# A four-layer graph network on one core: the row gathers unrolled on GpSimd, with a deeper ring in two layers

## The chip, the cores and the metric

The kernel runs on 1 core of one Trainium2 chip. The metric is device time in microseconds (us), from the runtime, for one execution. The engines have the names of the profile: PE (TensorE), DVE (VectorE), ACT (ScalarE), POOL (GpSimd) and SP (SyncE, which here only issues DMAs).

## The reference, cut to what matters

The graph has 6250 nodes of 128 float32 features and 106250 edges, sorted by destination. Four layers run one after the other, each on `h = relu(layernorm(x))`, and each adds its result to `x`:

```python
# layer 0: attention          per edge: k[src], v[src] (two rows of 128), q[dst]
a = einsum('eho,eho->eh', kw[src], q[dst]) * pri;  attn = softmax of a over the edges of a dst
h_agg = segment_sum(m * attn, dst)
# layer 1: degree-normalised  per edge: xs[src] (one row of 128)
h = segment_sum(xs[src], dst) * norm_out
# layer 2: gated              per edge: x[src] @ W_src and x[src] @ W_msg (two rows), edge_attr
gates = sigmoid(x_row @ W_src + x_col @ W_dst + edge_attr @ W_edge)
out = segment_sum(x_row @ W_msg * gates, dst) / segment_sum(gates, dst)
# layer 3: mean (SAGE)        per edge: x[src] (one row of 128)
summed = segment_sum(x[src], dst)
```

## The kernel before, in words

The edges lie in `T` = 896 tiles of 128 edges; every tile holds edges of one block of 128 destination nodes. Four tiles are a group (`QUAD`), so there are `NQ` = 224 groups. The node tables that are read per edge lie in device memory: `tab2` with rows of 1024 bytes (layers 0 and 2, the stages `scores` and `gated` in the code) and `tab1` with rows of 512 bytes (layers 1 and 3, the stages `degree` and `mean`).

In every layer POOL fetches the source rows: one indirect DMA for each tile (L500, 4 for a group, 896 for a layer, 3584 in all) takes 128 row numbers from a column of SBUF and brings 128 rows into the buffer `G`. `G` is a ring of `RING` = 4 groups. The row numbers of all tiles lie in `SRC`, one column for each tile; SP copies the four columns of a group by a small DMA into `ISLOT`, which has the same ring of 4 (L576, in layer 0 L596), and POOL names the columns of `ISLOT`. So before the gathers of group q POOL waits for the copy (`idx_filled`, L494), for the reader of the slot to be done with group q-4 (`rows_read`, L495), and in layer 0 for the store of the slot's second half (`mv_stored`, L497).

The loops of a layer's groups are made by `steps`: the first 8 groups and the last 8 are written out, those between run in a loop (`Fori`) whose body is 8 groups. Layer 0 has its own `layer0_steps`, which lets the messages of a group follow its scores 40 groups later, and has 7 hooks, one after every 32 groups, in which DVE works out the running maxima (`maxima`).

What reads the gathered rows: in `scores` DVE multiplies the first half of the rows with the spread q (L1257), and SP stores the second half (v) to `mvd` in device memory (L593) and loads it back into `MV` when the messages are due (L604; DVE weighs it, L1264). In `degree` and `mean` PE reads the rows directly: DVE makes a one-hot matrix for each tile (L971), PE multiplies it with the rows (L688, `pe_agg`), and DVE adds the four results to the accumulator of the block (L988). In `gated` DVE adds the first half (L1339) and multiplies the second half with the gate (L1331), then PE and DVE aggregate as before. The order in every engine's queue is written by hand, and all waits are semaphores. In `degree` DVE also makes two bf16 one-hots (L947, L951) for a histogram that PE sums (L702).

SP's queue, in order: in layer 0 for each step first the wait for the gathers of group q-4, their store to `mvd` and the index copy of group q, then the load of `MV`; in `degree` and `mean` only index copies, behind the loads of the next layer's weights (L645 to L648, L656 to L660); in `gated` the index copy and four loads of edge attributes (L580) for each group.

Of the kernel before, what the change touches and what calls it, by code (L numbers as in the profile page):

```python
# [7 lines left out]
I32 = mybir.dt.int32  # L8
# [13 lines left out]
RING = 4  # L22
UNROLL = 8
# [38 lines left out]
def build(nc, sz, a):  # L62
# [3 lines left out]
    with ctx:  # L66
        def sb(name, shape, dt=F32):
            return ctx.enter_context(nc.sbuf_tensor(name, shape, dt))

        def sem(name):  # L70
            return ctx.enter_context(nc.semaphore(name))
# [26 lines left out]
        ISLOT = sb("ISLOT", [P, RING, QUAD], I32)  # L98
# [27 lines left out]
        G1 = G[:, 0:RING * QUAD * D].rearrange("p (r j d) -> p r j d", r=RING, j=QUAD)  # L126
# [12 lines left out]
        def edge_sems(n):  # L139

            s = {"onehot_ready": sem(f"onehot_ready_{n}")}
            if n != "scores":
                s |= {k: sem(f"{k}_{n}") for k in ("agg_done", "rows_added")}
            if n != "messages":
                s |= {k: [sem(f"{k}{r}_{n}") for r in range(RING)] for k in ("idx_filled", "gathered")}
            return s
# [4 lines left out]
        def at(i, u, d):  # L151

            v = u + d
            i = i + v // UNROLL if v // UNROLL else i
            v %= UNROLL
            return i * UNROLL + v, v % RING, i * (UNROLL // RING) + v // RING, v

# [331 lines left out]
        def pool_gathers(pool, n, rows, table):  # L489
            s = ps[n]  # L490

            def step(i, u):
                q, slot, turn, _ = at(i, u, 0)
                pool.wait_ge(s["idx_filled"][slot], (turn + 1) * 16)  # L494
                wait(pool, rows_read[n], q - RING + 1)  # L495
                if n == 0:
                    wait(pool, mv_stored[slot], turn * 16)  # L497
                pool.sem_inc(may_gather, 1)
                for j in range(QUAD):
                    nc.gpsimd.indirect_dma_start(  # L500
                        out=rows[:, slot, j, :], out_offset=None, in_=table,
                        in_offset=bass.IndirectOffsetOnAxis(ap=ISLOT[:, slot, j:j + 1], axis=0),
                    ).then_inc(s["gathered"][slot], 16)
            steps(pool, step, 0)
# [64 lines left out]
        def sp_edges(sp, n):  # L569

            s = ps[n]

            def step(i, u):
                q, slot, turn, _ = at(i, u, 0)
                wait(sp, s["gathered"][slot], turn * 64)
                sp.dma_start(ISLOT[:, slot, :], SRC[:, bass.ds(q * QUAD, QUAD)]).then_inc(s["idx_filled"][slot], 16)  # L576
                if n == 3:
                    wait(sp, gated["pre_done"], q - RING + 1)
                    for j, first in enumerate(registers(sp, SROW, q, sz.edge_end)):
                        sp.dma_start(EA[:, slot, j, :], a["ea_t"][:, bass.ds(first, P)]).then_inc(ea_loaded[slot], 16)  # L580
            steps(sp, step, 0)

        def sp_layer0(sp):

            s = ps[0]

            def step(i, u, scores, messages):
                q, slot, turn, _ = at(i, u, 0)
                if scores:
                    wait(sp, s["gathered"][slot], turn * 64)  # L590
                    if not isinstance(q, int) or RING <= q < NQ + RING:
                        sp.sem_inc(may_move, 1)
                        sp.dma_start(mvd[bass.ds(q - RING, 1), :, :].rearrange("o p (j d) -> (o p) j d", j=QUAD),  # L593
                                     G2[:, slot, :, D:2 * D]).then_inc(mv_stored[slot], 16)
                    if valid(q):
                        sp.dma_start(ISLOT[:, slot, :], SRC[:, bass.ds(q * QUAD, QUAD)]).then_inc(s["idx_filled"][slot], 16)  # L596
                if messages:
                    q, slot, turn, _ = at(i - LAG, u, 0)
                    if valid(q):
                        sp.wait_ge(mv_stored[slot], (turn + 1) * 16)  # L600
                        sp.sem_inc(may_move, 1)
                        wait(sp, weighted["weighted"], q - RING + 1)
                        sp.sem_inc(may_move, 1)
                        sp.dma_start(MV[:, slot, :, :].rearrange("p j d -> p (j d)"),  # L604
                                     mvd[bass.ds(q, 1), :, :].rearrange("o p f -> (o p) f")).then_inc(mv_loaded[slot], 16)

            def guarded(i, u, scores, messages):
                step(i, u, scores and not (isinstance(i, int) and i == sz.iters and u >= RING), messages)
            layer0_steps(sp, guarded)
# [5 lines left out]
        def _(sp):  # L615
# [33 lines left out]
            sp_edges(sp, 2)  # L649
# [4 lines left out]
            sp_edges(sp, 3)  # L654
# [6 lines left out]
            sp_edges(sp, 4)  # L661
# [29 lines left out]
        def pe_plain(pe, n):  # L691
# [3 lines left out]
            def step(i, u):  # L695
# [8 lines left out]
                pe.wait_ge(s["gathered"][slot], (turn + 1) * 64)  # L704
                pe_agg(pe, n, q, slot, v % 2, lambda j: G1[:, slot, j, :], D)
# [721 lines left out]
```

## Time and profile before

| | us |
|---|---|
| median of 3 runs | 5664.36 |
| lowest and highest | 5662.23, 5675.72 |
| span of the profiled execution | 6742.5 |
| busy in it: POOL, DVE, PE, ACT | 3636.2, 3229.3, 3183.9, 663.9 |

The profiled execution is one execution under the hardware profiler; of its own time the page gives the span alone, from the first to the last instruction. It is 1078 us longer than the median of the runs without it. Each digit below is the busy share of 1/40 of the span in tenths; `PEclk` is TensorE's granted clock in tenths of full speed. The four stages with gathers are where POOL's digits are high.

```profile
PE   4534445444453333333426777677775133333333
DVE  6345665666785434343455444444446422322225
POOL 3465555555601666666653555555553366666661
PEclk9767676766766555555558888888887555555556
DMA  2345445555521111111223444444443111111131
```

### The profile page before, as it was taken

How to read it: one execution, taken by the hardware profiler on the slowest of the kernel's cores; microseconds unless marked ns; L12 is line 12 of the kernel's file. 1: busy time of each engine (PE TensorE's matmuls, PEld its weight loads, DVE VectorE, ACT ScalarE, POOL GpSimd, SP SyncE). 2: the span in 40 equal slices, each digit the busy share in tenths (PEclk: the TensorE clock that was granted, in tenths of full speed). 3: DMA queues.
4: the chain of work that ended last, by engine and by line, in shares of the span. 5: the costliest groups of instructions: out<-in, count | busy, mean ns of one | idle time of the engine just before them, and what ended most of it. 6: DMA issues, size and time to landing. Idle time of an engine off the chain costs nothing. (4 is left out here: it accounts for less than half of the span.)

```text
span 6742.5 us, 78555 instructions
## 1 busy us (share of the span) xinstructions
PE 3183.9 (47%) x16832; PEld 2674.3 (40%) x16833; DVE 3229.3 (48%) x7806; ACT 663.9 (10%) x1525; POOL 3636.2 (54%) x3680
## 2 busy tenths in 40 slices
PE   4534445444453333333426777677775133333333
PEld 2324444443343333333324666566664122332322
DVE  6345665666785434343455444444446422322225
ACT  3111111111102000000001111111111000000002
POOL 3465555555601666666653555555553366666661
PEclk9767676766766555555558888888887555555556
DMA  2345445555521111111223444444443111111131
GB/s 66 103 128 152 142 138 152 144 140 141 126 59 31 44 46 44 46 45 45 45 29 107 112 114 115 113 113 114 113 111 75 49 45 44 46 45 45 46 45 27
DMA packets 598120, 563.89 MB, mean 84 GB/s; under 512 B 215476, under 2 KB 480350, under 8 KB 598016
## 3 DMA queue, kind: packets, MB, share of 16 engines
q0 software_dynamic: 145888, 355.31, 20.5%
q1 hardware_dynamic: 452128, 207.41, 12.3%
q8 instruction: 38, 0.62, 0.0%
q14 instruction: 66, 0.54, 0.0%
HBM read 478.69 MB, written 81.82 MB: 83 GB/s over the span
## 5 line engine op out<-in xcount | busy, mean ns | idle before, releaser
L500 POOL DMA_INDIRECT G<-tab,ISLOT x3584 | 3503.4, 978 | 2817.0 <-issue 1253.7
L988 DVE TENSOR_TENSOR ACCR<-ACCR,PSA 128x128 f32 (+2 forms) x3584 | 1142.7, 319 | 2244.9 <-remote 1597.7
L688 PE MATMUL PSA<-G,S 128*128 128x128 f32 x3584 | 905.9, 432 | 1133.8 <-DMA G<-tab,ISLOT 550.4
L688 PEld LDWEIGHTS PSA<-G,S 128*128 128x128 f32 x3584 | 779.6, 321 | 1210.4 <-DVE ACCR L988 554.1
L971 DVE TENSOR_TENSOR S<-iota,REL 128x512 f32<-128x512 f32 x1120 | 790.0, 706 | 10.5 <-issue 7.1
L688 PE MATMUL PSA<-FLG,S 128*128 128x256 f32 x1792 | 552.2, 463 | 6.9 <-DVE FLG L1331 2.7
L1331 DVE TENSOR_TENSOR FLG<-G,FLG 128x512 f32<-128x512 f32 x224 | 155.1, 692 | 789.9 <-ACT FLG L927 542.9
L815 PE MATMUL PB<-QTR,ST 128*128 x1792 | 321.9, 336 | 400.6 <-ACT ST L834 388.8
L679 PE MATMUL PB<-identb,S 128*128 128x128 bf16 x1792 | 206.1, 247 | 618.9 <-DVE S L971 402.0
L815 PEld LDWEIGHTS PB<-QTR,ST 128*128 128x128 f32 x1792 | 280.2, 238 | 417.1 <-issue 416.5
L688 PEld LDWEIGHTS PSA<-FLG,S 128*128 128x128 f32 x1792 | 408.8, 240 | 88.2 <-issue 16.6
L834 ACT CAST ST<-PB 128x512 f32<-128x512 bf16 x448 | 262.1, 585 | 1784.4 <-remote 895.2
L679 PEld LDWEIGHTS PB<-identb,S 128*128 128x128 bf16 x1792 | 139.4, 111 | 714.5 <-DVE S L971 460.8
L702 PE MATMUL PB<-SCR 128*128 128x50 bf16 x896 | 77.6, 218 | 730.1 <-DVE SCR L951 606.0
L688 PE MATMUL PSA<-SCR,S 128*128 128x137 f32 x1792 | 348.9, 352 | 92.0 <-DVE ACCR L988 71.2
L761 PE MATMUL PB<-QTR,ST 128*128 x1792 | 353.2, 358 | 39.2 <-issue 33.9
L702 PEld LDWEIGHTS PB<-SCR 128*128 128x128 bf16 x896 | 51.2, 116 | 788.6 <-DVE SCR L951 643.8
L688 PEld LDWEIGHTS PSA<-SCR,S 128*128 128x128 f32 x1792 | 317.6, 255 | 100.6 <-DVE SCR L1264 66.5
L761 PEld LDWEIGHTS PB<-QTR,ST 128*128 128x128 f32 x1792 | 306.1, 258 | 76.3 <-issue 76.0
L811 PE MATMUL PB<-W,SCR 128*128 128x128 f32 x1792 | 255.0, 286 | 42.9 <-issue 36.1
L811 PEld LDWEIGHTS PB<-W,SCR 128*128 128x128 f32 x1792 | 220.8, 194 | 62.4 <-issue 57.3
L392 ACT COPY G<-PB 128x384 f32<-128x384 f32 (+2 forms) x200 | 79.7, 398 | 1623.2 <-PE PB L374 1623.2
(241 smaller groups left out, 2688.8 us busy)
## 6 DMA issues: line engine op xcount, KB each, us to landing
G<-tab,ISLOT POOLq DMA_INDIRECT x3584
mvd<-G SPq DMA_DIRECT2D x224, 256.0 KB
MV<-mvd SPq DMA_DIRECT2D x224, 256.0 KB
SCR<-in_ea_t SPq DMA_DIRECT2D x896, 64.0 KB
ISLOT<-SRC SPq DMA_DIRECT2D x896, 2.0 KB
tab<-G SPq DMA_DIRECT2D x100, 128.0 KB, 1.7
tab<-H SPq DMA_DIRECT2D x2, 3200.0 KB, 13.8
out_x<-X SPq DMA_DIRECT2D x1, 3072.0 KB
```

The source lines that it names most:

```text
L392: nc.scalar.copy(HT[:, r, 0:ni, :].rearrange("p t d -> p (t d)"), PB[r][:, 0:ni * P]).then_inc(s["copied"], 1)
L500: nc.gpsimd.indirect_dma_start(out=rows[:, slot, j, :], out_offset=None, in_=table, in_offset=bass.IndirectOffsetOnAxis(ap=ISLOT[:, slot, ...
L679: last = nc.tensor.transpose(STP[par][:, j, :], bf_view(slot, j), identb[:, :])
L688: last = nc.tensor.matmul(PSA[:, par, j, 0:width], S[:, slot, j, :], rhs(j), start=True, stop=True)
L702: nc.tensor.matmul(HISTP, LOH[:, slot, j, :], HIH[:, slot, j, :], start=first, stop=final, skip_group_check=True)
L761: last = nc.tensor.matmul(QD[v % 2][:, j, :], ST[:, v % 2, j, :], QT[:, bass.ds(blocks[j], 1), :].rearrange("p o d -> p (o d)"), start=Tru ...
L811: nc.tensor.matmul(QD[v % 2][:, j, :], EA[:, slot, j, :], W[:, 4 * D:5 * D], start=j == 0, stop=False, skip_group_check=True)
L815: last = nc.tensor.matmul(QD[v % 2][:, j, :], ST[:, v % 2, j, :], QT[:, bass.ds(blocks[j], 1), :].rearrange("p o d -> p (o d)"), start=Fal ...
L834: nc.scalar.copy(ST[:, par, :, :], STP[bank]).then_inc(s["st_copied"], 1)
L971: return v_.tensor_tensor(S[:, slot, :, :], bc(iota[:, :], [P, QUAD, P], 1), REL[:, bass.ds(q * QUAD, QUAD)].unsqueeze(2).to_broadcast([P, ...
L988: v_.tensor_tensor(rows, rows, PSA[:, par, j, 0:width], ALU.add).then_inc(s["rows_added"], 1)
L1331: v_.tensor_tensor(RHS[:, v % 2, :, 0:D], G2[:, slot, :, D:2 * D], RHS[:, v % 2, :, D:2 * D], ALU.mult).then_inc(s["multiplied"], 1)
```

## The change

`ISLOT`, its 896 copies by SP and the semaphores `idx_filled` are gone: a gather names its column of `SRC` directly. For that the loop over groups on POOL is written out in full (`for q in range(NQ)`), since the column must be a constant of the instruction; the waits then stand against constants, and the first groups of a ring have none. In `degree` and `mean` the ring of gathered rows has `DEEP` = 8 groups in the same buffer `G`, of which they used half before; the one-hots stay in a ring of 4, PE waits for `gathered[deep]`, and `scores` and `gated` keep 4. SP has nothing per group left in `degree` and `mean` (its calls of `sp_edges` are gone), in `gated` only the loads of edge attributes and no wait for gathers. In layer 0 a step of SP is turned round: first the load of `MV`, then the wait for the gathers of group q itself and their store to `mvd`, instead of those of group q-4.

```diff
+DEEP = 8
...
-        ISLOT = sb("ISLOT", [P, RING, QUAD], I32)
...
-        G1 = G[:, 0:RING * QUAD * D].rearrange("p (r j d) -> p r j d", r=RING, j=QUAD)
+        G1 = G[:, :].rearrange("p (r j d) -> p r j d", r=DEEP, j=QUAD)
...
-                s |= {k: [sem(f"{k}{r}_{n}") for r in range(RING)] for k in ("idx_filled", "gathered")}
+                s["gathered"] = [sem(f"gathered{r}_{n}") for r in range(DEEP if n in ("degree", "mean") else RING)]
...
         def pool_gathers(pool, n, rows, table):
             s = ps[n]
-
-            def step(i, u):
-                q, slot, turn, _ = at(i, u, 0)
-                pool.wait_ge(s["idx_filled"][slot], (turn + 1) * 16)
-                wait(pool, rows_read[n], q - RING + 1)
-                if n == 0:
-                    wait(pool, mv_stored[slot], turn * 16)
-                pool.sem_inc(may_gather, 1)
+            ring = len(s["gathered"])
+            for q in range(NQ):
+                slot, turn = q % ring, q // ring
+                if turn:
+                    pool.wait_ge(rows_read[n], q - ring + 1)
+                    if n == 0:
+                        pool.wait_ge(mv_stored[slot], turn * 16)
+                    pool.sem_inc(may_gather, 1)
                 for j in range(QUAD):
+                    k = q * QUAD + j
                     nc.gpsimd.indirect_dma_start(
                         out=rows[:, slot, j, :], out_offset=None, in_=table,
-                        in_offset=bass.IndirectOffsetOnAxis(ap=ISLOT[:, slot, j:j + 1], axis=0),
+                        in_offset=bass.IndirectOffsetOnAxis(ap=SRC[:, k:k + 1], axis=0),
                     ).then_inc(s["gathered"][slot], 16)
-            steps(pool, step, 0)
...
-        def sp_edges(sp, n):
+        def sp_edge_rows(sp):
             def step(i, u):
                 q, slot, turn, _ = at(i, u, 0)
-                wait(sp, s["gathered"][slot], turn * 64)
-                sp.dma_start(ISLOT[:, slot, :], SRC[:, bass.ds(q * QUAD, QUAD)]).then_inc(s["idx_filled"][slot], 16)
-                if n == 3:
-                    wait(sp, gated["pre_done"], q - RING + 1)
...
+                wait(sp, gated["pre_done"], q - RING + 1)
...
         def sp_layer0(sp):
             def step(i, u, scores, messages):
+                q, slot, turn, _ = at(i - LAG, u, 0)
+                if messages and valid(q):
+                    sp.wait_ge(mv_stored[slot], (turn + 1) * 16)
+                    sp.sem_inc(may_move, 1)
+                    wait(sp, weighted["weighted"], q - RING + 1)
...
                 q, slot, turn, _ = at(i, u, 0)
-                if scores:
-                    wait(sp, s["gathered"][slot], turn * 64)
...
+                if scores and valid(q):
+                    sp.wait_ge(s["gathered"][slot], (turn + 1) * 64)
+                    sp.sem_inc(may_move, 1)
+                    sp.dma_start(mvd[bass.ds(q, 1), :, :].rearrange("o p (j d) -> (o p) j d", j=QUAD),
+                                 G2[:, slot, :, D:2 * D]).then_inc(mv_stored[slot], 16)
...
-            sp_edges(sp, 2)
...
-            sp_edges(sp, 3)
+            sp_edge_rows(sp)
...
-            sp_edges(sp, 4)
...
-                pe.wait_ge(s["gathered"][slot], (turn + 1) * 64)
-                pe_agg(pe, n, q, slot, v % 2, lambda j: G1[:, slot, j, :], D)
+                _, deep, round_, _ = at(i, u, 0, DEEP)
+                pe.wait_ge(s["gathered"][deep], (round_ + 1) * 64)
+                pe_agg(pe, n, q, slot, v % 2, lambda j: G1[:, deep, j, :], D)
```

## Rows read from the trace of the kernel before

**Rows 1.** Windows view, line L500 alone: window, its length, POOL busy (instructions), clock, DMA.

```profile
0.00:226.00 226.00, 0.00 (x0) 0.96 0.23 64
226.00:1804.00 1578.00, 884.25 (x896) 0.69 0.52 142
1804.00:2160.00 356.00, 0.00 (x0) 0.66 0.16 45
2160.00:3477.00 1317.00, 897.71 (x896) 0.52 0.20 45
3477.00:3617.00 140.00, 0.00 (x0) 0.72 0.16 48
3617.00:5169.00 1552.00, 857.73 (x896) 0.83 0.45 114
5169.00:5296.00 127.00, 0.07 (x2) 0.56 0.13 31
5296.00:6603.00 1307.00, 863.68 (x896) 0.51 0.21 45
6603.00:6742.50 139.50, 0.00 (x0) 0.68 0.10 24
...
2160.00:2252.00 92.00, 62.09 (x64) 0.54 0.19 45
```

**Rows 2.** Groups by line on POOL: gathers from small index tile, direct DMAs, window gathers.

```profile
L500 POOL DMA_INDIRECT G<-tab,ISLOT x3584 | 3503.4, 978 | 2817.0 <-issue 1253.7 <-DMA ISLOT<-SRC 608.8 <-DVE FLG L1331 329.9
L530 POOL DMA_DIRECT2D FLG<-flagd x56 | 29.8, 600 | 38.9 <-DMA metad<-QTR 38.9
L521 POOL DMA_INDIRECT G<-in_dst_win,QTR x7 | 6.6, 946 | 2.1 <-issue 2.1
```

**Rows 3.** Timeline of `degree`: start, us, instruction, idle before it and releaser.

```profile
2252.67 1.09 POOL L500 DMA_INDIRECT G<-tab,ISLOT  x1 [0.30 <-issue]
...
2708.76 2.07 PE L688 MATMUL PSA<-G,S 128*128 128x128 f32 x8
...
2718.93 0.29 DVE L988 TENSOR_TENSOR ACCR<-ACCR,PSA 128x128 f32 x1 [10.33 <-remote]
...
2719.57 1.07 POOL L500 DMA_INDIRECT G<-tab,ISLOT  x1 [4.11 <-remote]
...
2721.84 0.69 DVE L971 TENSOR_TENSOR S<-iota,REL 128x512 f32<-128x512 f32 x1
...
2724.54 0.69 DVE L971 TENSOR_TENSOR S<-iota,REL 128x512 f32<-128x512 f32 x1
```

**Rows 4.** Timeline of DVE in `scores` and `gated`: two pairs of successive groups.

```profile
1240.95 0.68 DVE L1257 TENSOR_TENSOR SCR<-G,PB 128x512 f32<-128x512 f32 x1
...
1244.78 0.68 DVE L1257 TENSOR_TENSOR SCR<-G,PB 128x512 f32<-128x512 f32 x1
...
3918.71 0.69 DVE L1331 TENSOR_TENSOR FLG<-G,FLG 128x512 f32<-128x512 f32 x1 [2.73 <-issue]
...
3922.93 0.69 DVE L1331 TENSOR_TENSOR FLG<-G,FLG 128x512 f32<-128x512 f32 x1 [0.77 <-issue]
```

**Rows 5.** Timeline of POOL in `scores`: gathers behind a hook, the first and the longest of six.

```profile
494.44 1.30 POOL L500 DMA_INDIRECT G<-tab,ISLOT  x1 [10.82 <-DVE SCR L1257]
...
1195.89 0.95 POOL L500 DMA_INDIRECT G<-tab,ISLOT  x1 [22.47 <-DVE SCR L1257]
```

**Rows 6.** Timeline, begin of `degree` and of `mean`; last, DMA issues with us to landing.

```profile
2143.20 0.38 SPq L645 DMA_DIRECT2D tab<-H  x1
...
2160.14 0.99 POOL L500 DMA_INDIRECT G<-tab,ISLOT  x1 [293.18 <-DMA ISLOT<-SRC]
...
5278.21 0.39 SPq L656 DMA_DIRECT2D tab<-H  x1
...
5296.00 0.94 POOL L500 DMA_INDIRECT G<-tab,ISLOT  x1 [126.93 <-DMA ISLOT<-SRC]
...
tab<-H SPq DMA_DIRECT2D x2, 3200.0 KB, 13.8
```

More of the change, by code:

```diff
@@ L149, in build, with at @@
         reg_note = "computed on the chip from the tile's position, always in range"
-        def at(i, u, d):
+        def at(i, u, d, ring=RING):
             v = u + d
@@ L155, in at @@
             v %= UNROLL
-            return i * UNROLL + v, v % RING, i * (UNROLL // RING) + v // RING, v
+            return i * UNROLL + v, v % ring, i * (UNROLL // ring) + v // ring, v
         def valid(q):
@@ L566, in _ @@
             pool_gathers(pool, 4, G1, tab1)
-        def sp_edges(sp, n):
-            s = ps[n]
+        def sp_edge_rows(sp):
             def step(i, u):
                 q, slot, turn, _ = at(i, u, 0)
-                wait(sp, s["gathered"][slot], turn * 64)
-                sp.dma_start(ISLOT[:, slot, :], SRC[:, bass.ds(q * QUAD, QUAD)]).then_inc(s["idx_filled"][slot], 16)
-                if n == 3:
-                    wait(sp, gated["pre_done"], q - RING + 1)
-                    for j, first in enumerate(registers(sp, SROW, q, sz.edge_end)):
-                        sp.dma_start(EA[:, slot, j, :], a["ea_t"][:, bass.ds(first, P)]).then_inc(ea_loaded[slot], 16)
+                wait(sp, gated["pre_done"], q - RING + 1)
+                for j, first in enumerate(registers(sp, SROW, q, sz.edge_end)):
+                    sp.dma_start(EA[:, slot, j, :], a["ea_t"][:, bass.ds(first, P)]).then_inc(ea_loaded[slot], 16)
             steps(sp, step, 0)
@@ L587, in step @@
             def step(i, u, scores, messages):
-                q, slot, turn, _ = at(i, u, 0)
-                if scores:
-                    wait(sp, s["gathered"][slot], turn * 64)
[L591 to L605, printed above, removed]
@@ L607, in guarded @@
-            def guarded(i, u, scores, messages):
-                step(i, u, scores and not (isinstance(i, int) and i == sz.iters and u >= RING), messages)
-            layer0_steps(sp, guarded)
+                q, slot, turn, _ = at(i - LAG, u, 0)
[4 more added lines that the diff above has]
+                    sp.sem_inc(may_move, 1)
+                    sp.dma_start(MV[:, slot, :, :].rearrange("p j d -> p (j d)"),
+                                 mvd[bass.ds(q, 1), :, :].rearrange("o p f -> (o p) f")).then_inc(mv_loaded[slot], 16)
@@ L611, in row_bc @@
+                q, slot, turn, _ = at(i, u, 0)
+                if scores and valid(q):
+                    sp.wait_ge(s["gathered"][slot], (turn + 1) * 64)
+                    sp.sem_inc(may_move, 1)
+                    sp.dma_start(mvd[bass.ds(q, 1), :, :].rearrange("o p (j d) -> (o p) j d", j=QUAD),
+                                 G2[:, slot, :, D:2 * D]).then_inc(mv_stored[slot], 16)
+            layer0_steps(sp, step)
         def row_bc(v, n):
```

## The prediction

> **What bounds the kernel now.** I read the windows view first, for the gathers alone [rows 1]. The reader is to see nine windows: four in which POOL issues 896 gathers each (1578, 1317, 1552 and 1307 us, together 5754 us) and five without gathers (226 + 356 + 140 + 127 + 139.5 = 988.5 us). The two make up the span of 6742.5 us.
>
> Then the groups by line [rows 2]. A gather is busy for 0.945 us where nothing disturbs it; the mean of 978 ns holds 3503.4 - 3584 x 0.945 = 117 us of longer ones, which overlap with DVE's work. Behind every gather stands a gap of 0.30 us that the view calls issue, also where POOL waits for nothing [rows 3]. So POOL's own pace is 1.25 us for a gather, 5.0 us for a group, 1120 us for a layer, 4480 us for all four. The windows hold more than that: 5754 - 3503 - 3584 x 0.305 = 1158 us in which POOL stands still.
>
> Then the timeline, for what it waits on there. In `degree` [rows 3] PE starts the matmuls of a group at 2708.76, DVE sees that they are done at 2718.93 after 10.33 us idle with the releaser "remote", and POOL, whose ring of 4 is full, comes out of its wait at 2719.57. Once PE answers, DVE takes a group in 2721.84 to 2724.54 = 2.7 us. In `scores` and `gated` undisturbed groups follow each other after 3.83 and 4.22 us [rows 4]. So whoever reads the rows needs less than POOL's 5.0 us, and only these standstills of PE stop POOL.
>
> **Are the standstills in the timed runs?** The whole prediction hangs on this, since the profiled execution takes 6742.5 us and the median of the timed runs is 5664.36, 1078 us less. Two readings fit. Reading A: POOL's 1.25 us is real, and the standstills belong to the profiled execution. One kind of wait is real in any case: at six of the hooks of layer 0 DVE is away for so long that POOL idles 10.8 to 22.5 us [rows 5], 65 to 135 us in sum. That gives 988.5 + 4480 + 117 + 65 to 135 = 5650 to 5720 us, and the median lies in it with nothing fitted. Reading B: the gap of 0.30 us comes from recording, and the standstills are real: 988.5 + 3503 + 1158 = 5650 us. The sum doesn't tell them apart, so a row must. The 56 direct DMAs that POOL issues at L530 are recorded in the same way and have no gap: their 38.9 us idle is one wait at the start [rows 2]. The gather of L521 has the same 0.30 us (2.1 us for 7). The gap thus belongs to the indirect DMA and not to the recording. I take A, and POOL's pace as the bound in all four layers.
>
> **The index copies go.** Removed are 896 copies by SP, and one wait of POOL for each group. While the ring turns they cost nothing now: a copy starts when the gathers of q-4 have landed, some 15 us ahead of its use at 5 us a group, and SP has room. Naming a column of a wide tile directly costs the gather nothing either: L521 does so with its index tile, in 0.946 us and with the same gap [rows 2].
>
> At the beginning of `degree` and `mean` the copy does end last, since it stands in SP's queue behind the six (then five) loads of weights. The table's store is issued at 2143.20 and lands 13.8 us later, at 2157.0; POOL starts at 2160.14. In `mean` it is 5278.21 + 13.8 = 5292.0 against 5296.00 [rows 6]. From a released wait to the gather pass about 0.6 us (2718.93 to 2719.57, [rows 3]). So 2.5 and 3.4 us go, 6 us in sum, and there the landing of the table is late next. In `scores` and `gated` the copy is issued right behind the last table store and lands at about the same time: nothing. Bounds of the part: 0 and the 7.1 us of both differences.
>
> **POOL's loop is written out.** Removed are the branch and register work at each turn of the loop, every 32 gathers. They are hidden: behind the 64 gathers of [rows 1] (2160 to 2252), where the body turns, the next one starts at 2252.67 with the usual 0.30 us [rows 3]. POOL's sequencer works ahead of the gathers that still run. Added are 3584 gathers and up to two waits for each of 896 groups, some 5,000 instructions, in one long stream that must be fetched as it runs. The trace has only short straight stretches on POOL: 56 direct DMAs without a gap, and the first 32 gathers of each stage at the same pace. The bounds are thus 0 and one fetch that isn't hidden for each such stretch of 56: 3584 / 56 = 64 times the 0.945 us of one gather, 60 us. I take 0, the row's value.
>
> The Trainium skill (Runtime: NRT & Kernel Launch, Instruction fetch mechanics) says that a taken branch out of the two resident pages forces a fetch before execution goes on, and prefers unrolling for it. The trace shows no such fetch at 2252.67. By the page's 16 KiB blocks of 256 instructions (an estimate from that page) the new stream has about 20 block borders, which the page calls mostly hidden.
>
> **The ring of 8.** Under A the reader of the rows is faster than POOL (2.7 us for 5.0), so a deeper ring is never used in a timed run: 0. It covers the head of a stage too, but in `degree` and `mean` the first one-hots are ready before the first rows land. In the profiled execution the ring pays: POOL's idle time over its pace is 1317 - 898 - 273 = 146 us in `degree` and 1307 - 864 - 273 = 170 us in `mean` [rows 1], 316 us, and one standstill of some 10 us now meets 40 us of stored work in place of 20. This is also the upper bound of the gain, should the standstills be real.
>
> **SP in layer 0.** The store of group q to `mvd` is issued as soon as the gathers of q have landed, and no longer waits behind an `MV` load that waits for DVE. The load of `MV` now stands behind the store of the group before it, so it can't run four groups ahead as before. It is needed one group and about 1 us later, some 5.5 us after its issue. Were it late, DVE would start its group later by a constant, while POOL still has its ring; the hooks stay as they are, with a ring of 4. I take 0. The 114,688 packets of the copies (896 x 128) leave DMA queues that are busy 16 to 52% of the time [rows 1]: nothing on the path.
>
> **Sum.** -6 (heads) + 0 + 0 + 0. Against the profiled execution's own time the sum is 6742.5 - 6 - most of 316, so I expect its span at about 6450 us (6380 to 6600). The timed runs should show only the 6 us: 5664 - 6 = 5658 us.
>
> **The rivals.**
> Reading B, the standstills are real. For it: they are long and regular in the trace, and 5650 us fits as well. Against: the direct DMAs without a gap, and that B needs a POOL pace of just 0.978 us by coincidence. The ring would give back up to 316 us: 5664 - 6 - 316 = 5342 us; DVE and PE, at 2.7 us a group plus 10 us every five to six groups (some 4.6 us a group against POOL's 3.9), would become the bound of the two layers, so about half, 5500 us. A weaker form, with a few real standstills that a ring of 4 doesn't cover, gives 20 to 70 us: 5590 to 5640.
>
> Slower: the fetch of POOL's stream. Its place is POOL in all four layers, its price 0.945 us for each of 64 stretches, 60 us, minus the 6: 5718 us. It decides from the point where a refill takes longer than the gathers that are queued ahead. For it: POOL never ran more than some hundred instructions straight. Against: no gap at any straight stretch. A half-hidden form gives 5680.
>
> The change doesn't do what it says: the start of `degree` and `mean` is held by the landing of the table just as long, since POOL's wait for it also ends late. Then 5664 us, within the same class.
>
> **Chances.** What a measurement of this kernel can tell from no change is about 0.3%, 17 us: 5647 to 5681. A or the last rival: 0.57. A few real standstills: 0.16. Reading B in full: 0.09. The fetch: 0.14, of which 0.03 ends within 17 us. The rest, 0.04, is other slowdown. Of A, 0.03 goes to a gain just over 17 us. Faster 0.16 + 0.09 + 0.03 = 0.28; slower 0.11 + 0.04 = 0.15; same 0.57 - 0.03 + 0.03 = 0.57. The range leaves out B in full, the stronger end of the fetch and some of the rest: 5590 to 5705 us; the likeliest case alone is 5645 to 5668.
>
> **What would show it.** After: POOL's first gather of `degree` and `mean` starts 2 to 4 us sooner behind the table's store; gathers stand 1.25 us apart through the whole stream, with no new gap at a regular count of instructions; in `degree` and `mean` the waits of POOL for "remote" shrink from 134 and 150 us to under 50 each; the hooks' gaps stay at 11 to 22 us. The profiled span falls far more than the time does. The prediction is wrong if the time falls about as much as the span (B), or if the windows of `degree` and `mean` without standstills are longer than 1120 us plus the longer gathers (the fetch).

## The result

The changed kernel takes 5696.45 us (median of 4 runs, 5692.05 to 5696.9) and the kernel before 5666.57 us beside it (4 runs, 5662.23 to 5675.72). The ratio is 1.0046, with a 95% interval of 1.0030 to 1.0061. The forecast was 5658 us, six us faster; the kernel became 30 us slower.

The profiled execution of the changed kernel has a span of 5690.2 us and a time of 5692.05 us. That is a surprise by itself: the span shown of the kernel before was 6742.5 us. The kernel before was profiled again beside the experiments (e10): that execution took 5666.59 us with a span of 5664.8 us and has none of PE's standstills, the waits of some 10 us for PE as in [rows 3]. This is the trace to compare with.

The windows view, POOL's gathers alone, answers to [rows 1] (window, its length, POOL busy with its instructions, clock, DMA share, GB/s). First the kernel before, of e10:

```profile
226.40:1469.30 1242.90, 915.57 (x896) 0.75 0.67 181
1824.40:3010.60 1186.20, 913.45 (x896) 0.50 0.23 50
3151.30:4282.70 1131.40, 858.65 (x896) 0.99 0.61 156
4402.50:5524.00 1121.50, 848.78 (x896) 0.50 0.24 53
```

Then the changed kernel:

```profile
225.40:1454.00 1228.60, 907.69 (x896) 0.75 0.66 182
1808.00:2992.50 1184.50, 911.76 (x896) 0.50 0.22 50
3133.10:4311.50 1178.40, 905.76 (x895) 0.97 0.57 149
4427.70:5548.60 1120.90, 848.16 (x895) 0.51 0.23 53
```

`scores` became 14.3 us shorter, `degree` 1.7 and `mean` 0.6, and `gated`, the third row, became 47.0 us longer, all of it in gathers that take longer (858.65 to 905.76 us busy). In the groups by line it is the mean duration of a gather that moved. The kernel before of e10, then the changed kernel [rows 2]:

```profile
L500 POOL DMA_INDIRECT G<-tab,ISLOT x3584 | 3540.0, 988 | 1706.8 <-issue 919.6 <-DMA ISLOT<-SRC 594.9 <-PE PSA L688 89.3
```

```profile
L501 POOL DMA_INDIRECT G<-tab,SRC x3584 | 3577.1, 998 | 1693.2 <-issue 1339.3 <-DMA tab<-G 146.2 <-DMA tab<-H 115.2
```

The sum closes: 37.1 us more busy, 6.6 us less idle in `scores` (idle time over the usual gap, summed over its gathers: 54.6 and 48.0, nearly all right behind the hooks), 5.9 us less in the stretches ahead of the four stages, 0.7 more behind the last. Together 25.3 us, of 25.4 between the spans.

### The profile page after: what moved, and what is told of

It is laid out like the page before. It is cut to its first block, busy times and chain, and to the rows that moved or that the text cites. A ratio compares the mean times of both kernels' runs of the same rounds, so it can differ in the third digit from the quotient of the medians.

```text
span 5690.2 us, 75333 instructions
## 1 busy us (share of the span) xinstructions
PE 3000.8 (53%) x16832; PEld 2526.1 (44%) x16833; DVE 3253.1 (57%) x7806; ACT 674.5 (12%) x1525; POOL 3709.3 (65%) x3680
## 3 DMA queue, kind: packets, MB, share of 16 engines
q0 software_dynamic: 145888, 355.31, 25.3%
## 4 chain that ended last, share of the span: by engine, by line
POOL 40%; issue 20%; DMA 16%; DVE 12%; PE 9%; ACT 2%; DVEq 1%; SPq 0%; POOLq 0%; ACTq 0%
POOL G L501 40%; DMA G<-tab,SRC 11%; DMA mvd<-G 4%; PE PB L381 3%; DVE ACCR L975 2%; PE PB L798 1%; DVE S L958 1%; PE PSA L674 1%; PE PB L802 1%; DVE ACCR L982 1%; PE PB L374 1%; ACT H L840 1%; PE PB L665 1%; DVE G L401 1%; DVE ACCR L1338 1%
## 5 line engine op out<-in xcount | busy, mean ns | idle before, releaser
L501 POOL DMA_INDIRECT G<-tab,SRC x3584 | 3577.1, 998 | 1693.2 <-issue 1339.3
L958 DVE TENSOR_TENSOR S<-iota,REL 128x512 f32<-128x512 f32 x1120 | 797.5, 712 | 4.2 <-issue 0.5
L674 PE MATMUL PSA<-FLG,S 128*128 128x256 f32 x1792 | 435.5, 386 | 7.9 <-DVE FLG L1318 6.7
L665 PEld LDWEIGHTS PB<-identb,S 128*128 128x128 bf16 x1792 | 115.5, 105 | 641.3 <-DVE S L958 602.6
L748 PE MATMUL PB<-QTR,ST 128*128 x1792 | 355.1, 360 | 51.8 <-issue 47.1
L674 PE MATMUL PSA<-SCR,S 128*128 128x137 f32 x1792 | 324.5, 337 | 67.5 <-DVE ACCR L975 67.4
L674 PEld LDWEIGHTS PSA<-FLG,S 128*128 128x128 f32 x1792 | 328.5, 194 | 48.8 <-DVE FLG L1318 9.1
L748 PEld LDWEIGHTS PB<-QTR,ST 128*128 128x128 f32 x1792 | 303.7, 256 | 93.4 <-issue 93.4
L1244 DVE TENSOR_TENSOR SCR<-G,PB 128x512 f32<-128x512 f32 x224 | 153.8, 686 | 263.5 <-DMA G<-tab,SRC 112.5
L1326 DVE TENSOR_TENSOR SCR<-PB,G 128x512 f32<-128x512 f32 x224 | 154.8, 691 | 203.5 <-issue 122.8
L802 PE MATMUL PB<-QTR,ST 128*128 x1792 | 250.5, 285 | 0.0
L381 PE MATMUL PB<-W,G 128*128 128x128 f32 (+2 forms) x900 | 236.2, 392 | 0.7 <-DVE G L401 0.7
```

Source lines behind the costliest of these rows:

```text
L381: last = nc.tensor.matmul(PB[2 + (1 - r)][:, 0:cols], HT[:, 1 - r, t, :], w(t), start=t == 0, stop=t == ni - 1)
L501: nc.gpsimd.indirect_dma_start(out=rows[:, slot, j, :], out_offset=None, in_=table, in_offset=bass.IndirectOffsetOnAxis(ap=SRC[:, k:k + 1] ...
L665: last = nc.tensor.transpose(STP[par][:, j, :], bf_view(slot, j), identb[:, :])
L674: last = nc.tensor.matmul(PSA[:, par, j, 0:width], S[:, slot, j, :], rhs(j), start=True, stop=True)
L748: last = nc.tensor.matmul(QD[v % 2][:, j, :], ST[:, v % 2, j, :], QT[:, bass.ds(blocks[j], 1), :].rearrange("p o d -> p (o d)"), start=Tru ...
L802: last = nc.tensor.matmul(QD[v % 2][:, j, :], ST[:, v % 2, j, :], QT[:, bass.ds(blocks[j], 1), :].rearrange("p o d -> p (o d)"), start=Fal ...
```

## Where a gather gets longer

The timeline of `gated` shows it (start, duration, instruction, idle before it and its releaser). Here the kernel before, of e10, from the last gather of one group to the last of the next:

```profile
3700.88 0.94 POOL L500 DMA_INDIRECT G<-tab,ISLOT  x1 [0.30 <-issue]
...
3702.13 0.95 POOL L500 DMA_INDIRECT G<-tab,ISLOT  x1 [0.30 <-issue]
3702.57 0.69 DVE L1331 TENSOR_TENSOR FLG<-G,FLG 128x512 f32<-128x512 f32 x1 [0.75 <-ACT FLG L927]
...
3704.20 0.69 DVE L1339 TENSOR_TENSOR SCR<-PB,G 128x512 f32<-128x512 f32 x1 [0.60 <-DMA G<-tab,ISLOT]
3704.31 0.52 SPq L576 DMA_DIRECT2D ISLOT<-SRC  x1
...
3705.51 1.84 SPq L580 DMA_DIRECT2D SCR<-in_ea_t  x4
...
3705.88 0.95 POOL L500 DMA_INDIRECT G<-tab,ISLOT  x1 [0.30 <-issue]
```

A group begins at 3702.13 and its last gather at 3705.88. The gate multiplication (L1331) begins 0.44 us behind the beginning of a gather, and both take their usual time. The rows of the gather of 3700.88, the last of its group, let the pre-sum (L1339) go at 3704.20, 3.32 us later. SP issues the edge rows at 3705.51, beside the last gather. The changed kernel at the same place:

```profile
3709.37 0.94 POOL L501 DMA_INDIRECT G<-tab,SRC  x1 [0.30 <-issue]
...
3710.62 0.95 POOL L501 DMA_INDIRECT G<-tab,SRC  x1 [0.30 <-DVE FLG L1318]
3711.54 1.82 SPq L575 DMA_DIRECT2D SCR<-in_ea_t  x4
...
3712.17 0.69 DVE L1326 TENSOR_TENSOR SCR<-PB,G 128x512 f32<-128x512 f32 x1 [1.26 <-issue]
...
3715.48 0.69 DVE L1318 TENSOR_TENSOR FLG<-G,FLG 128x512 f32<-128x512 f32 x1 [0.74 <-ACT FLG L914]
3715.62 1.37 POOL L501 DMA_INDIRECT G<-tab,SRC  x1 [0.30 <-issue]
```

The edge rows leave 0.9 us behind the group's beginning (3710.62). The pre-sum comes 2.80 us behind the last gather's beginning (3709.37), and the multiplication follows the pre-sum after 3.3 us (median 3.26 in both traces). Seen from the last gather of a group, gathers that nothing lengthens begin 5.0 and 6.25 us later. With a pre-sum at 2.8 the multiplication falls at about 6.1 us, just ahead of the second of these; with 3.3 it falls at about 6.6, inside it. So here it begins 0.14 us ahead of a gather, not behind one, and this gather takes 1.37 us in place of 0.95. The one-hot comparison (L958, both inputs in SBUF too), 0.94 us behind the pre-sum, moves in the same way from the inside of the third gather of a group to its beginning.

Over all groups of `gated` in the changed kernel the same numbers come out. With the multiplication (two inputs in SBUF, 693 ns) beginning 0.1 to 0.2 us ahead of a gather, the gather is 432 ns longer on the mean (76 cases); at 0.4 to 0.5 us ahead, 120 ns (3 cases); beginning within a running gather, 0 to 2 ns (136 cases). So a gather that begins under such an operation waits for about what is left of it, less 0.1 us; where the operation began less than 50 ns ahead it mostly waits for nothing (34 of 37 cases), and an operation that begins under a gather costs nothing. The pre-sum, which reads one input from PSUM, has no such effect: 1 ns in 41 cases at the same offset. The rule holds in all four layers: of the 625 gathers of the changed kernel that took over 990 ns, 624 began under a DVE operation with both inputs in SBUF, and none under one that reads PSUM. In `gated` the multiplication and the one-hot share the blame, with 37.8 and 21.4 us.

The Trainium skill (SBUF — State Buffer, section SBUF: two separate sides) describes an exclusive lock on a port pair of DVE and GpSimd, which DVE takes with two SBUF inputs against a GpSimd operation that reads SBUF, and which whoever starts first holds for the whole instruction. The traces agree on who waits; they don't bear out that a gather holds the pair for its whole length, since the multiplication of 3702.57 ran its usual 0.69 us inside a gather.

Both kernels show either pattern in places. The kernel before has 36 lengthened gathers (13.3 us), nearly all in its first 20 and last 30 groups; the changed kernel has 180 of them (60.5 us), from end to end. Long groups don't follow each other there: of the groups 25 to 199, 87 took over 5.2 us (5.54 on the mean) and the others about 5.0, and behind 67 of the 87 stands a short one. The stage goes back and forth between the two.

## The experiments

The theories that the expectations name: L, lengthened gathers are real time. P, later D: in `gated` the removed copies moved SP's edge rows, and with them DVE, against the gathers. The rivals: F, the fetch of the written-out stream; R, the deeper ring; S, SP's new order in layer 0; M, the loss lies outside the gathers; Q, POOL's own waiting for copies kept the beginnings free. Two are on the standstills: K, the index copies cause them; C, they belong to the chip. M is answered by the sum above: the stretches without gathers became shorter, by 5 us together.

**POOL's loop written out, copies kept** (the kernel before, otherwise):

```diff
-            def step(i, u):
-                q, slot, turn, _ = at(i, u, 0)
+            for q in range(NQ):
+                slot, turn = q % RING, q // RING
```

> The kernel before, with nothing changed but that POOL's loop over groups is written out; the index copies by SP, their ring of 4 and all other queues stay. The change cost 30 us (5666.6 to 5696.5). Theory L (lengthened gathers): POOL is the bound, and the loss is in gathers that run while DVE holds two inputs from SBUF; writing out the loop changes nothing of the phase between POOL and DVE, so about 5667 us, within 8. Rival F (the fetch of the long stream): the whole loss comes with the written-out loop, so about 5696 us. If the index copies are what disturbs the profiled execution, its span is again far above the time, 6500 us or more.

> The kernel before with POOL's loop written out and nothing else changed, now on a chip without standstills. Theory L: as long as the kernel before within 8 us, since the phase between POOL and DVE stays. Rival F (fetch of the long stream): the whole 26 to 30 us. On the other chip it was 0.9986 (0.9978 to 0.9995) of the kernel before.

> The kernel before with POOL's loop written out and nothing else. On a chip without standstills theory L expects the kernel before within 8 us, rival F (fetch of the long stream) 26 to 30 us more. With standstills (6820 us) it tells nothing of the 30 us.

Measured: 6809.58 against 6818.2 us (0.9986, interval 0.9978 to 0.9995), 6823.19 against 6825.72 (0.9992, 0.9981 to 1.0002), 5664.49 against 5664.73 (0.9997, 0.9985 to 1.0008). The first two met PE's standstills, which are told of below; the third is the plain case. 896 gathers a layer in one straight stream cost nothing: F is out.

**Ring of 4 in the changed kernel**:

```diff
-DEEP = 8
+DEEP = 4
...
-        G1 = G[:, :].rearrange("p (r j d) -> p r j d", r=DEEP, j=QUAD)
+        G1 = G[:, 0:DEEP * QUAD * D].rearrange("p (r j d) -> p r j d", r=DEEP, j=QUAD)
```

> The changed kernel with a ring of 4 groups in `degree` and `mean` in place of 8. In the trace of the changed kernel POOL never waits in these two layers, and the readers need 2.7 us of its 5 us for a group, so both the theory of lengthened gathers and that of the fetch expect no difference: 5696 us, within 5. Rival R (the ring lets POOL run over more of DVE's work or spreads its writes): the two layers give back part of the 30 us, 5670 to 5690 us.

Measured: 6773.53 against 6818.2 us (0.9936, 0.9922 to 0.9950), with standstills; the kernel of the next experiment, with a ring of 8 but also SP's old order in layer 0, took 6776.71 beside it. The windows of `degree`, ring of 4, then ring of 8:

```profile
2206.40:3515.60 1309.20, 900.00 (x896) 0.51 0.19 45
```

```profile
2202.60:3515.10 1312.50, 899.99 (x896) 0.53 0.19 45
```

So the deeper ring gives nothing even there. It does fill: where POOL stops in `degree`, PE is two groups behind it with a ring of 4 and six with a ring of 8 (medians over 43 stops each). With 8 it is always at least four groups behind, so it hardly ever runs out of rows, and the 5.86 us a group that the stage takes are PE's own pace with its standstills. A ring can't make up for that. Without standstills a ring of 4 was not run, so R is not tested there; POOL has no wait to save in those layers, and their windows in the changed kernel are 1.7 and 0.6 us shorter, not longer.

**SP's old order in layer 0**, without its index copies; the load of `MV` follows, and the rest is as changed:

```diff
...
-                    sp.wait_ge(s["gathered"][slot], (turn + 1) * 64)
...
-                    sp.dma_start(mvd[bass.ds(q, 1), :, :].rearrange("o p (j d) -> (o p) j d", j=QUAD),
...
+                    wait(sp, s["gathered"][slot], turn * 64)
...
+                        sp.dma_start(mvd[bass.ds(q - RING, 1), :, :].rearrange("o p (j d) -> (o p) j d", j=QUAD),
...
```

> The changed kernel with SP's steps in layer 0 in the old order: store of group q-4, then the load of `MV`, no index copy. Rival S (the new order is what costs): the gathers of `scores` are longer by 62 us in sum after the change; with the old order the time falls by up to 30 us, to 5666 to 5680. The theory that the loss lies in gathers lengthened by DVE in several layers expects a part of that at most: 5685 to 5697 us. The fetch expects 5696 us.

> The changed kernel with SP's steps in layer 0 in the old order (store of group q-4 before the load of `MV`). Rival S: it gives back up to 30 us against the changed kernel's 5696. Theory L expects only the part of `scores`: 5685 to 5697 us.

> The changed kernel with SP's old order in layer 0. On a chip without standstills rival S expects 5666 to 5680 us, theory L 5685 to 5697 us, the fetch 5696 us. With standstills 0.993 of the kernel before, as on two chips.

Measured: 6776.71 against 6818.2 us (0.9938, 0.9924 to 0.9953), 6776.12 against 6825.72 (0.9927, 0.9905 to 0.9949), 5706.89 against 5664.73 (1.0071, 1.0048 to 1.0094). S is out: the new order is no loss but worth 5 to 8 us in `scores` (window 1236.2 us in e12; 1228.6 in the changed kernel and up to 1231.3 in the other kernels with the new order). K is out too: this kernel has no index copy, and PE stood still in e3 and e8.

**Counting row in PSUM**: the changed kernel, but the one-hot comparisons of `degree` and `mean` read it from PSUM:

```diff
+        IOTAP = PB[0][:, 3 * P:4 * P]
...
-                return v_.tensor_tensor(S[:, slot, :, :], bc(iota[:, :], [P, QUAD, P], 1),
+                return v_.tensor_tensor(S[:, slot, :, :], bc(IOTAP if n in (2, 4) else iota[:, :], [P, QUAD, P], 1),
...
```

The two bf16 one-hots of `degree` are changed in the same way, and DVE copies the row into PSUM ahead of each of the two layers.

> The changed kernel, but in `degree` and `mean` DVE's comparisons for the one-hots read the counting row from PSUM in place of SBUF, so they have one SBUF input and not two. Theory L: gathers of `degree` are longer by 66 us in sum only where they overlap with these operations; this goes nearly whole, `degree` is 1125 us from first to last gather in place of 1184, and the time is about 5635 us (5625 to 5650). If the gathers are lengthened by something else (DMA traffic, the fetch of the stream), the time stays at 5696 us and the mean gather of `degree` at 1.02 us.

> The changed kernel, but in `degree` and `mean` the comparisons for the one-hots read the counting row from PSUM. On the chip with standstills the lengthening of the gathers of `degree` fell by this from about 54 us to 0.8 us and POOL's waits grew by as much. Here nothing makes POOL wait, so theory L expects the whole 66 us back: about 5630 us (5622 to 5645), faster than both kernels. If the time stays at 5696, POOL isn't the bound of `degree`.

> The changed kernel with the counting row of `degree` and `mean` read from PSUM. On a chip without standstills theory L expects about 5630 us (5622 to 5645), faster than both kernels, since POOL bounds and 66 us of lengthened gathers go; the other theories 5696 us. With standstills 0.998 of the kernel before, as on two chips.

Measured: 6801.76 against 6818.2 us (0.9982, 0.9970 to 0.9993), 6814.65 against 6825.72 (0.9972, 0.9957 to 0.9987), 5624.4 against 5664.73 (0.9926, 0.9897 to 0.9955). The last is 72 us under the changed kernel's median of the first comparison, and the windows of `degree` and `mean` are 71 us shorter together. Timeline of `degree`, first the changed kernel, then e13:

```profile
2405.80 0.69 DVE L934 TENSOR_TENSOR SCR<-iota,FLG 128x512 bf16<-128x512 f32 x1
2406.00 1.30 POOL L501 DMA_INDIRECT G<-tab,SRC  x1 [0.30 <-issue]
```

```profile
2403.28 0.68 DVE L935 TENSOR_TENSOR SCR<-PB,FLG 128x512 bf16<-128x512 f32 x1
...
2403.68 0.94 POOL L502 DMA_INDIRECT G<-tab,SRC  x1 [0.30 <-issue]
```

The operation takes as long as before and no longer holds the gather. No gather of `degree` is lengthened now (220 before), and its window is POOL's bare pace:

```profile
1809.40:2926.60 1117.20, 844.43 (x895) 0.50 0.23 53
3066.20:4248.20 1182.00, 909.21 (x895) 0.98 0.56 149
```

The second row is `gated`, which this kernel leaves as it was. L holds where POOL is the bound. Under standstills the same edit gives nothing: e4 and e9 took 25 and 39 us more than e3 and e8, which differ from them in SP's order of layer 0 too; why is not known.

**The two kernels again**:

> The changed kernel itself, one look beside the kernel before on the same chip. On the chip of e1 to e4 the kernel before took 6818 us with the standstills of TensorE in its trace, where the timed runs of the comparison took 5667 us and the changed kernel's trace of 5690 us has no standstill. Theory C (the standstills belong to the chip and not to the kernel or to the recording): either both kernels are near 6800 us with standstills, the changed one some 0.5% faster, or both are near 5680 us without them. Rival K (the index copies bring the standstills about): the changed kernel is near 5690 us wherever it runs.

> The kernel before, unchanged, for a trace of it on a chip without standstills (if this chip is one). Theory L (the loss lies in gathers lengthened by DVE): from first to last gather `scores`, `degree` and `gated` hold about 30 us less of lengthened gathers together than after the change (62 + 66 + 60 us), with no idle of POOL but at the hooks. Rival M (the loss is outside the gathers, in the messages' tail of layer 0 or a projection): the gathers are lengthened as much as after, and a window without gathers is 30 us shorter.

> The kernel before, unchanged, for its trace on a chip without standstills, if this is one. Theory L (the loss lies in gathers lengthened by DVE): `scores`, `degree` and `gated` hold about 30 us less of lengthened gathers together than after the change (62 + 66 + 60 us); POOL idles at the hooks alone. Rival M: they are lengthened as much, and a window without gathers is 30 us shorter.

Measured: the changed kernel 5695.74 against 5670.35 us (one run each); the kernel before 6835.12 against 6825.72 with standstills, and 5666.54 against 5664.73 without (1.0004, 0.9992 to 1.0015). The standstills come with the kernel before and with variants of the changed one, and both also run without them, so they belong to neither kernel. Nor do they belong to a chip for good, as C has it: one chip gave both kinds (e1 to e4, then e10 to e13).

**The wait for landed gathers given back to SP in `gated`**, alone (e14) and with the PSUM row (e15):

```diff
                 q, slot, turn, _ = at(i, u, 0)
+                wait(sp, ps[3]["gathered"][slot], turn * 64)
+                sp.sem_inc(may_move, 1)
                 wait(sp, gated["pre_done"], q - RING + 1)
```

> The changed kernel with one wait given back in `gated`: before it loads the edge rows of group q, SP waits again until the gathers of group q-4 have landed, as the removed index copies made it do; no copies, no other edit. Theory P (phase): the +30 us is all in `gated`, where the changed kernel's gathers were lengthened by 60.5 us in 180 places against 13.3 us in 36 places in the kernel before. A gather is lengthened only where a DVE operation with two SBUF inputs is under way as it begins, by what is left of that operation; the edge rows now leave 2 to 4 us earlier in a group of gathers (SP's issues at 0.5 to 3 us of the 5 us, before at 3 to 5), and the score and gate operations of DVE fall half a microsecond earlier, across the beginnings of gathers. P expects with the wait: `gated` from first to last gather 1131 to 1140 us (changed kernel 1178.4), lengthening under 20 us, time 5645 to 5655. Rival Q (the index copies themselves, their transfers or POOL's waiting for them, set the phase): `gated` stays at 1178 us and the time at 5690 to 5700. Should PE stand still as in some of the runs, the time is near 6775 by both and nothing is told apart.

> The same wait, and the counting row read from PSUM by the one-hot comparisons of `degree` and `mean` (which took `degree` from 1184.5 to 1117.2 us and `mean` from 1120.9 to 1117.2). By P the two gains add: `gated` 1131 to 1140 us, time 5575 to 5590, below both kernels. By Q it is 5624, as without the wait. If the phase in `gated` hangs on something that the layers ahead pass on, the gain in `gated` comes out different from that of the run beside it.

Measured: 5705.96 against 5666.55 us (1.0075, 1.0052 to 1.0098) and 5625.2 against 5666.55 (0.9926, 0.9897 to 0.9955). P in this form fell: the wait keeps nothing away, `gated` was even longer. Its window in e14:

```profile
3130.00:4323.70 1193.70, 918.46 (x893) 0.98 0.56 148
```

What the trace of e14 left was one difference: its edge rows start at 2.2 us of a group, against 3.2 in the kernel before and 1.5 in the changed one (medians over groups 25 to 199, here and below). The last landing of a group comes 2.80 us behind its last gather's beginning in e14 and 2.75 in the changed kernel, and 3.22 in the kernel before.

**Edge rows late again**: e16 (first diff, without the lines that make `ISLOT` and its semaphores) adds to e14 an index copy that no gather reads; e17 (second) has neither the copy nor that wait, but waits for the one-hot of group q-2.

```diff
+                wait(sp, idx_filled[slot], turn * 16)
+                sp.sem_inc(may_move, 1)
                 wait(sp, ps[3]["gathered"][slot], turn * 64)
+                sp.dma_start(ISLOT[:, slot, :], SRC[:, bass.ds(q * QUAD, QUAD)]).then_inc(idx_filled[slot], 16)
```

```diff
+                wait(sp, ps[3]["onehot_ready"], q - 1)
```

> The wait of e14 and, behind it, an index copy that no gather reads, so that SP's edge-row issues start at about 3 us of a group of gathers, as in the kernel before (3.2), and not at 1.0 to 1.7 (changed kernel) or 2.2 (e14). Theory D (edge rows against the last gather): where the edge rows are issued beside the last gather of a group, that gather's rows land late, and the pre-sum of DVE begins 3.3 us after that gather begins (kernel before), not 2.82 (changed) or 2.88 (e14); then the gate multiplication begins just behind the beginning of a gather and not just ahead of it. D expects pre-sum at 3.15 to 3.35 us, lengthening in `gated` under 25 us, `gated` 1130 to 1143 us, time 5645 to 5662. Rival Q (POOL's waiting for the copies set the phase in the kernel before): 2.8 us, 1178 to 1194 us, 5690 to 5706.

> No copy and no wait for gathers: SP waits until DVE has made the one-hot tile of group q-2 before it loads the edge rows of group q, which puts its four issues at about 3.7 to 6 us of a group of gathers, later still than in the kernel before. D expects the pre-sum at 3.1 us or later behind the last gather's beginning and `gated` at 1130 to 1150 us, time 5645 to 5670; if it is the copies in any form that matter, 2.8 us, 1178 us or more and 5690 to 5706.

Measured: 6731.02 against 6741.44 us (0.9986, 0.9968 to 1.0003) and 6715.61 against 6741.44 (0.9959, 0.9932 to 0.9986). PE stood still in both, so the times tell nothing of the theories. The traces don't show what D expected either: the last landing of a group comes 2.71 us behind its last gather's beginning in both, and in e17 with edge rows issued beside that gather as soon as without (2.65 us in 114 groups with one issue, 2.73 in 45 with two, 2.72 in 63 with none).

**e16 with the PSUM row**:

> e16 (in `gated` SP waits for the gathers of group q-4, issues an index copy that no gather reads, then the edge rows) together with e13 (counting row from PSUM in `degree` and `mean`). It asks what e16 could not answer while PE stood still. Theory D (edge rows issued beside the last gather of a group make its rows land later, and so keep DVE's operations off the beginnings of gathers): edge rows first issued at about 3.0 us of a group, pre-sum 3.15 to 3.35 us behind the last gather's beginning, lengthening in `gated` under 25 us, `gated` 1130 to 1143 us; with `degree` at 1117 the time is 5575 to 5592, under both kernels. Rival Q (what kept them off in the kernel before was POOL's own waiting for the copies, or the copies' being read): pre-sum at 2.8 us, `gated` 1178 to 1194 us, 5624 to 5640. Should PE stand still again, the time is near 6750 by both and the question stays open.

Measured: 5573.63 against 5660.06 us (0.9845, 0.9816 to 0.9873). Windows of e18, `degree` and `gated`:

```profile
1809.30:2926.60 1117.30, 844.47 (x896) 0.50 0.23 53
3066.50:4200.80 1134.30, 861.50 (x896) 0.98 0.60 156
```

Its timeline in `gated`:

```profile
3600.44 0.95 POOL L504 DMA_INDIRECT G<-tab,SRC  x1 [0.30 <-issue]
...
3601.69 0.95 POOL L504 DMA_INDIRECT G<-tab,SRC  x1 [0.30 <-issue]
3602.09 0.69 DVE L1326 TENSOR_TENSOR FLG<-G,FLG 128x512 f32<-128x512 f32 x1 [0.75 <-ACT FLG L921]
...
3605.01 1.83 SPq L582 DMA_DIRECT2D SCR<-in_ea_t  x4
...
3605.44 0.94 POOL L504 DMA_INDIRECT G<-tab,SRC  x1 [0.30 <-issue]
...
3608.76 0.69 DVE L1334 TENSOR_TENSOR SCR<-PB,G 128x512 f32<-128x512 f32 x1 [0.64 <-PE PB L809]
```

The edge rows stand beside the last gather again (3605.01 and 3605.44), the pre-sum comes 3.32 us behind it, the multiplication 0.40 us behind the beginning of a gather, and nothing is lengthened here. In the whole stage 42 gathers are, by 16.3 us. e15 and e18 differ by the copy alone, which no gather reads: 1183.9 and 1134.3 us in `gated`, 5625.2 and 5573.6 in time. So Q fell, and D has its step: the issue of the edge rows beside the last gather delays that gather's rows (last landing 3.19 us behind its beginning), and this decides where DVE falls.

The copy was the means to delay the edge rows here, but the changed kernel, which has no copy, shows the same step in those groups whose edge rows leave late. Counted are issues of edge rows from 0.5 us ahead of the last gather's beginning to 1.5 us behind it: with none the last landing comes after 2.74 us (median of 166 groups), with one after 3.00 (29 groups), with two to four after 3.49 (29 groups). And over all traces without standstills `gated` takes 1131 to 1135 us from first to last gather in the three kernels whose edge rows leave at 3.2 us of a group (e10, e11, e18) and 1179 to 1195 in the others. What stays open is the condition: where PE stood still (e16, e17) the edge rows delayed nothing, and no edit that moves them without a copy was run without standstills. And in e10 and e18 the view names PE's projection as the last releaser of the pre-sum more often (106 of 191, 105 of 185) than the landing (70, 66); its end, 2.65 us behind that beginning on the median in both, is earlier than the landing, and the pre-sum begins 0.08 us behind the last landing on the median in all of these traces, so I hold to the landing.

## Why the prediction was wrong, by its steps

- **The bound.** Right: POOL's 1.25 us a gather sets all four stages. The bare windows of 1117.2 us in e13 are 896 times 1.247.
- **Reading A.** Half right. The timed runs that were shown had no standstills, and A's sum holds for them, though by terms that were off both ways. In e10 they are 979 us without gathers, 4479 of pace, 153 of longer gathers (forecast 117) and 55 of waits in `scores` (forecast 65 to 135; the longest is 8.8 us, not 22.5), together 5666 for a span of 5665. But the standstills don't belong to the profiled execution. Where a profile has them, the timed runs beside it take 6818 us (e1 to e4) or 6826 (e6 to e9) as well. The trace and the median of before came from executions of different kinds.
- **Index copies, at the heads.** Right in kind and in sum. In the changed kernel the table's store is issued and the first gathers begin at

```profile
1792.30 0.38 SPq L633 DMA_DIRECT2D tab<-H  x1
1807.98 0.99 POOL L501 DMA_INDIRECT G<-tab,SRC  x1 [292.71 <-issue]
...
4414.51 0.39 SPq L643 DMA_DIRECT2D tab<-H  x1
4427.68 0.94 POOL L501 DMA_INDIRECT G<-tab,SRC  x1 [115.21 <-DMA tab<-H]
```

That is 15.68 and 13.17 us, for 16.92 and 17.99 in e10: 1.2 and 4.8 us gone where 2.5 and 3.4 were forecast. The sum of 6.0 is met because the two errors cancel.

- **Index copies, "while the ring turns they cost nothing".** This is the step that failed. In `gated` they cost nothing, but they also held SP's edge rows back to 3.2 us of a group. The prediction looked at what waited for the copies and not at what stood behind them in SP's queue.
- **The 117 us of longer gathers** were seen, put down to an overlap with DVE, and taken as fixed. They depend on where DVE's operations begin, and that moved: 13.3 to 60.5 us in `gated`. In the trace with standstills that stage had only 857.73 - 896 x 0.945 = 11 us of them [rows 1], and in e10 13.3, so no row of the kernel before gave a hint of what they could become. This term is +47 us for the 0 forecast.
- **The loop written out.** Right: 0 (e11).
- **The ring of 8.** 0 for the time fits, though no run without standstills tests it alone. Wrong for the span where PE stands still: the two layers should have given back most of 316 us, and `degree` took 1309.2 and 1312.5 us with 4 and 8. The 4.6 us a group that reading B gave PE and DVE were 5.86, more than POOL's 5.0.
- **SP in layer 0.** Forecast 0; `scores` gained 14.3 us, 5 to 8 of it by the order. The other 6.7 lie between e10 and e12, which has the old order but no copies; their removal was forecast at 0 there.
- **The rivals.** The fetch didn't come. B didn't come: without standstills the gap of 0.30 us is there behind every gather. Slower came by a mechanism that was not on the list. That 5696 us still lies in the range of 5590 to 5705 is luck: its upper part was there for the fetch.

## What to carry to other kernels

When an instruction is taken out of a queue, ask what stood behind it and moves forward, and what that will then collide or no longer collide with. Where POOL's indirect gathers are the bound, every DVE operation with both inputs in SBUF that is under way as a gather begins is paid for: put one input in PSUM (72 us here) or keep the operation off the beginnings. And take the trace and the time from the same execution before a sum is built on them.

## What the runs showed that was not expected

- **Two kinds of executions.** The kernel before takes 5656 to 5676 us or 6721 to 6843 us, the same kind for a whole series of runs on one chip; one chip gave the long kind in one series and the short in a later one. In the long kind PE answers late, as in [rows 3], and `scores` and `gated` each take some 330 to 450 us more. Which kernel is ahead depends on the kind: the changed kernel with the old order of SP is 0.6 to 0.7% faster than the kernel before there, and 0.7% slower in the short kind. What brings the standstills about was not found.
- **A gather meets DVE only at its beginning**: an operation that begins later within its 0.95 us costs nothing on either side (136 cases, 0 to 2 ns).
- **Half a microsecond decides over 47.** With the same work `gated` ran at 5.05 us a group or, on the mean of groups of 5.0 and 5.5, at 5.26 (1131.4 and 1178.4 us for 224), decided by 0.47 us in the landing of the last rows (3.22 and 2.75).
